# Target rows spread by one-hot products ahead of the edge scores, with the high one-hot rows on ScalarE

## The reference

```python
q = (node_features @ Wq.T + bq).reshape(N, H, D)
k = (node_features @ Wk.T + bk).reshape(N, H, D)
v = (node_features @ Wv.T + bv).reshape(N, H, D)
scores = jnp.sum(q[src] * k[dest], axis=-1) / jnp.sqrt(jnp.float32(D))
scores = scores + attention_mask
seg_max = jax.ops.segment_max(scores, src, num_segments=N)
ex = jnp.exp(scores - seg_max[src])
seg_sum = jax.ops.segment_sum(ex, src, num_segments=N)
weights = ex / seg_sum[src]
weighted = v[src] * weights[:, :, None]
out = jax.ops.segment_sum(weighted, dest, num_segments=N)
```

## Time and profile before

| what | value |
|---|---|
| median of 3 runs | 7013.81 us (7011.34 to 7027.35) |
| the profiled execution, its own time | 7010.85 us |
| its span, first to last instruction | 7009.2 us |
| granted TensorE clock over the span | 0.793 |
| busy: TensorE, VectorE, ScalarE, GpSimd | 4774.6, 4285.0, 2451.2, 4258.3 us |
| first to last instruction of the score stage | 4530.8 to 6053.6 us |

### The profile page before, as it was taken

One profiled execution on the slowest core, in us unless ns is written; L12 is line 12 of the kernel. 1 busy time (PEld: TensorE's weight loads), 2 busy tenths in 40 slices (PEclk: granted clock), 3 DMA queues, 4 the chain that ended last, 5 costly groups with the idle time before them and its releaser, 6 DMA issues. The chain is left out here.

```text
span 7009.2 us, 133354 instructions
## 1 busy us (share of the span) xinstructions
PE 4774.6 (68%) x26165; PEld 3739.8 (53%) x26166; DVE 4285.0 (61%) x13848; ACT 2451.2 (35%) x6084; POOL 4258.3 (61%) x4642
## 2 busy tenths in 40 slices
PE   3666666778868876546887767666666666346557
PEld 2555555557757765435764555444444444235545
DVE  4555556887635543863556757866666666665458
ACT  1555555325652125205313416711111111122149
POOL 3777773003575557667776775477777777347730
PEclk7777777999989988558999967977777777667579
DMA  1222223658969976976875536722222222123358
GB/s 29 72 75 73 74 73 110 196 168 297 342 207 302 314 253 210 343 247 207 268 227 180 179 96 232 248 74 69 70 72 69 69 72 69 49 81 115 85 181 289
DMA packets 616834, 1119.21 MB, mean 160 GB/s; under 512 B 124786, under 2 KB 133392, under 8 KB 616336
## 3 DMA queue, kind: packets, MB, share of 16 engines
q1 hardware_dynamic: 299984, 547.66, 23.3%
q10 hardware_dynamic: 183456, 334.05, 13.8%
q0 software_dynamic: 133280, 236.29, 12.7%
HBM read 675.98 MB, written 441.55 MB: 159 GB/s over the span
## 5 line engine op out<-in xcount | busy, mean ns | idle before, releaser
L520 PE MATMUL agg_bank<-agg_msgs,agg_onehot 128*128 x7840 | 1344.0, 325 | 541.9 <-DVE agg_onehot L450 423.6
L520 PEld LDWEIGHTS agg_bank<-agg_msgs,agg_onehot 128*128 128x128 f32 x7840 | 1161.7, 227 | 777.2 <-issue 773.1
L450 DVE TENSOR_TENSOR agg_onehot<-iota,rel 128x512 f32<-128x512 f32 x1176 | 809.9, 689 | 706.6 <-PE agg_bank L520 271.3
L368 POOL DMA_INDIRECT agg_msgs<-near,agg_rows x784 | 792.7, 1011 | 375.3 <-issue 205.5
L368 POOL DMA_INDIRECT agg_msgs<-y,agg_rows x784 | 784.6, 1001 | 261.6 <-issue 200.4
L564 ACT ACTIVATE agg_kept<-agg_bank 128x512 f32<-128x512 f32 x294 | 175.6, 597 | 1097.9 <-PE agg_bank L520 1084.0
L365 POOL DMA_INDIRECT agg_weight<-weights,agg_rows x392 | 410.7, 1048 | 124.4 <-issue 103.0
L520 PE MATMUL agg_bank<-agg_weighted,agg_onehot 128*128 x1568 | 339.5, 387 | 209.9 <-DVE agg_onehot L450 161.8
L1452 POOL DMA_INDIRECT mlp_xs<-in_x,mlp_rows x392 | 409.2, 1044 | 116.7 <-issue 115.8
L562 ACT ACTIVATE agg_kept<-agg_bank,inv_root 128x128 f32<-128x128 f32 x784 | 224.1, 369 | 721.2 <-PE agg_bank L520 672.1
L1748 POOL DMA_INDIRECT by_source<-score_line,score_places x392 | 389.3, 993 | 125.6 <-issue 117.4
(11 more groups left out here) (344 smaller groups left out, 11942.3 us busy)
## 6 DMA issues: line engine op xcount, KB each, us to landing
sums<-agg_kept ACTq DMA_DIRECT2D x490, 256.0 KB
agg_first<-start ACTq DMA_DIRECT2D x196, 256.0 KB
agg_first<-y ACTq DMA_DIRECT2D x196, 256.0 KB
messages<-mlp_m SPq DMA_DIRECT2D x98, 256.0 KB, 2.1
agg_first<-in_x ACTq DMA_DIRECT2D x98, 256.0 KB
agg_msgs<-messages SPq DMA_DIRECT2D x98, 256.0 KB
l_z<-sums SPq DMA_DIRECT2D x98, 256.0 KB
x<-l_o POOLq DMA_DIRECT2D x98, 256.0 KB
```

Source lines behind the costliest of these rows:

```text
L368: pool.indirect_dma_start(msgs[:, j, :], None, table[:, :], bass.IndirectOffsetOnAxis(ap=rows[:, third, j:j + 1], axis=0)).then_inc(sm[f"g ...
L450: nc.vector.tensor_tensor(onehot[:, j, :, :], k.iota[:, 0:P].unsqueeze(1).to_broadcast([P, Q, P]), k.rel[:, ds(i * (4 * Q) + j * Q, Q)].un ...
L520: t.matmul(bank[:, column[q], :], onehot[:, j, q, :], messages[:, slot[q], :], start=False, stop=True, skip_group_check=True)\
```

## The change

**Setup** also keeps the position of each edge in each step as a row in DRAM (`rel_rows`): TensorE transposes `k.rel` in seven pieces, VectorE copies them as bf16, SyncE stores them. Two more tables tell when an edge group is complete (`edge_done`) and when a node group's buffer is free (`node_left`).

**A new stage** `spread_rows` runs before the scores. It is an aggregation the other way round: it goes through the same 784 steps, with node rows as the loaded ring and edge tiles as the PSUM columns. The positions of a quad's edges are broadcast to all partitions by DMA (bf16, four quads at a time, 512 KB written), VectorE compares them with the partition number, TensorE multiplies the one-hot matrix with the node rows, and ScalarE stores the target row of every edge in a DRAM table. GpSimd, beside this, gathers the source rows of every fourth edge group into another DRAM table.

**The score stage** loads target rows, and the source rows of every fourth group, with plain DMAs on SyncE, ahead of its load of source numbers and of its store. GpSimd gathers sources in three of four groups only. The copy of the turned targets moves from VectorE to ScalarE. The high one-hot rows move from VectorE (one comparison a tile) to ScalarE (two activations a tile: the absolute difference, then Relu of one minus it), as the last step of ScalarE's round.

**Mean products** (`MeanProducts`): VectorE copies the turned rows before it keeps results, where it did so after.

```diff
@@ setup @@
+                sp.wait_ge(sm["rel_rows"], 2)
+                sp.dma_start(rel_rows.rearrange("a (j s e) -> s (a j) e", s=REL_ROWS, e=P), relT[:, :, :]).then_inc(sm["rel_out"], 16)
+                sp.wait_ge(sm["rel_out"], 16)
...
+                v.tensor_copy(relT[:, 0:4, :], pT[0:REL_ROWS, :, :]).then_inc(sm["rel_rows"], 1)
+                v.tensor_copy(relT[:, 4:7, :], pHT[0:REL_ROWS, 0:3, :]).then_inc(sm["rel_rows"], 1)
...
+                for j in range(STEPS // REL_ROWS):
+                    to = pT[0:REL_ROWS, j, :] if j < 4 else pHT[0:REL_ROWS, j - 4, :]
+                    t.transpose(to, k.rel[:, j * REL_ROWS:(j + 1) * REL_ROWS], k.ident[:, :]).then_inc(sm["turned_rel"], 1)
@@ MeanProducts @@
-            for lag, what in ((4, keep), (2, copy)):
+            for lag, what in ((2, copy), (4, keep)):
@@ spread_rows, GpSimd @@
+                    for q in range(Q):
+                        pool.indirect_dma_start(got[:, m, q, :], None, table[:, :], bass.IndirectOffsetOnAxis(
+                            ap=rows[:, m, q:q + 1], axis=0)).then_inc(sm[f"moved{m}"], 16)
+
+                def chunk(i, c):
+                    if not isinstance(i, int) or i * CHUNK + c >= 2:
+                        pool.wait_ge(sm["onehot"], i * (CHUNK * CHUNK) + (c - 1) * CHUNK)
+                    pool.sem_inc(sm["pass_pool"], 1)
+                    pool.dma_start(rel[:, c % 2, :, :], rel_rows[:, ds(i * (CHUNK * CHUNK * Q * P) + c * (CHUNK * Q * P), CHUNK * Q * P)]
+                                   .to_broadcast([P, CHUNK * Q * P])).then_inc(sm[f"rel{c % 2}"], 16)
+
+                def body(i):
+                    for c in range(CHUNK):
+                        chunk(i, c)
+                        if c % 2 == 0:
+                            copy_rows(i, c // 2)
+                        else:
+                            gather(i, c // 2)
...
@@ spread_rows, SyncE @@
+                def load(i, u):
+                    g = i * DEEP + u
+                    sp.wait_ge(sm["summed"], sp.value_load(k.node_left[0:1, ds(g, 1)], min_val=1, max_val=STEPS + SHIFT))
+                    sp.dma_start(nodes[:, u * Q:(u + 1) * Q, :], rows_of(table, g)).then_inc(sm[f"loaded{u}"], 16)
...
+                    for lag, step in ((0, load), (2, arrive)):
@@ spread_rows, VectorE @@
+                        dve.wait_ge(sm["arrived"], arrived)
...
+                        dve.wait_ge(sm["ready"], ready)
...
+                        dve.wait_ge(sm["summed"], i * (2 * CHUNK * Q) + ((c * CHUNK + j) * Q + 1))
+                        nc.vector.tensor_scalar(onehot[:, j, :, :], rel[:, c, j, :].rearrange("p (q e) -> p q e", q=Q), k.pid[:, 0:1], None, ALU.is_equal)\
+                          .then_inc(sm["onehot"], 1)
@@ spread_rows, TensorE @@
+                        pe.wait_ge(sm["onehot"], i * CHUNK + (j + 1))
+                        for q in range(Q):
+                            t.matmul(bank[:, column[q], :], onehot[:, j, q, :], nodes[:, slot[q], :], start=False, stop=True, skip_group_check=True)\
+                             .then_inc(sm["summed"], 1)
@@ spread_rows, ScalarE @@
+                    act.wait_ge(sm["summed"], act.value_load(k.edge_done[0:1, ds(g, 1)], min_val=1, max_val=STEPS + SHIFT))
+                    a.activation(kept[:, u, :, :], bank[:, u * Q:(u + 1) * Q, :], ACT.Copy).then_inc(sm["emptied"], 1)
...
+                        fill(u)
+                    act.dma_start(rows_of(out, g), kept[:, u, :, :]).then_inc(sm[f"written{u}"], 16)
@@ edge_scores, SyncE @@
+                    sp.dma_start(xd[:, u, :, :], rows_of(target_rows, g)).then_inc(sm[f"dst{u}"], 16)
+                    if u == DEEP - 1:
+                        sp.dma_start(xs[:, u, :, :], rows_of(source_rows, g)).then_inc(sm[f"src{u}"], 16)
...
-                    for lag, step in ((0, load_sources), (3, store)):
+                    for lag, step in ((0, load_rows), (0, load_sources), (3, store)):
@@ edge_scores, GpSimd @@
-                    for which, to, sem in ((0, xs, "src"), (1, xd, "dst")):
-                        for q in range(Q):
...
+                    for q in range(Q):
+                        pool.indirect_dma_start(xs[:, b, q, :], None, x3[:, :], bass.IndirectOffsetOnAxis(
+                            ap=rows[:, half, at + q:at + q + 1], axis=0)).then_inc(sm[f"src{b}"], 16)
...
-                        if live(*before_by(i, u, lag, TWICE), TWICE):
+                        if live(*before_by(i, u, lag, TWICE), TWICE) and (lag or u % DEEP < DEEP - 1):
@@ edge_scores, TensorE @@
                 def count(i, u):
+                    pe.wait_ge(sm["hot_hi"], i * DEEP + u + 1)
@@ edge_scores, ScalarE @@
+                    a.activation(xdT[:, u % 2, :, :], pDst[:, :, :], ACT.Copy).then_inc(sm["copied_dst"], 1)
...
+                def make_hot_hi(i, u):
...
+                    for q in range(Q):
+                        last = a.activation(apart[:, q, :], k.iota[:, 0:NT], ACT.Abs, bias=less_hi[:, ds(g * Q + q, 1)])
+                    last.then_inc(sm["apart"], 1)
+                    act.wait_ge(sm["apart"], g + 1)
+                    for q in range(Q):
+                        last = a.activation(hot_hi[:, u % 2, q, :], apart[:, q, :], ACT.Relu, scale=-1.0, bias=k.ones[:, 0:1])
+                    last.then_inc(sm["hot_hi"], 1)
+
                 def body(i, u):
                     for lag, step in ((0, round_off), (0, copy_source), (0, copy_lo), (1, keep)):
...
+                        make_hot_hi(*before_by(i, u, -1))
@@ edge_scores, VectorE @@
-                    v.tensor_copy(xdT[:, u % 2, :, :], pDst[:, :, :]).then_inc(sm["copied_dst"], 1)
...
-                        last = v.tensor_scalar(hot_hi[:, u % 2, q, :], k.iota[:, 0:NT], k.src_hi[:, ds(g * Q + q, 1)], None, ALU.is_equal)
+                        last = v.tensor_scalar(hot_lo[:, u % 2, q, :], k.iota[:, 0:P], k.src_lo[:, ds(g * Q + q, 1)], None, ALU.is_equal)
```

More of the change, by code:

```diff
@@ L1650, in edge_scores @@
+def edge_scores(nc, k, ins, x3, source_rows, target_rows, values, by_source):
+    sm = phase(nc, "score", ["mask", "w", "spread", "rows", "pass_pool", "pass_sp", "turned", "copied_src", "copied_dst", "product", "kept",
                              "multiplied", "reduced", "scored",
-                             "constants", "c", "begun", "hot", "leant", "copied_lo", "rounded", "rest", "looked", "selected", "ranked", "placed", "moved", "counted"] + [f"{s}{u}" for s in ("src", "dst", "stored", "scattered", "line_of") for u in range(DEEP)])
+                             "constants", "c", "begun", "hot", "apart", "hot_hi", "leant", "copied_lo", "rounded", "rest", "looked", "selected", "ranked", "placed", "moved", "counted"] + [f"{s}{u}" for s in ("src", "dst", "stored", "scattered", "line_of") for u in range(DEEP)])
@@ L1964, in body @@
                     if live(*now):
-                        copy_target(*now)
                         take_rest(*now)
```

202 lines of the change are left out of this document (172 added, 30 removed).

## The result

The changed kernel takes 7287.05 us (median of 4 runs, 7281.99 to 7294.84) against 7012.58 for the kernel before: a ratio of 1.0385, 95% interval 1.037 to 1.0401. It is slower, as forecast, but by 274 us and not by 72, and above the range. The profiled execution spans 7293.3 us, 284 more than that of before.

A forecast was written before the change was run, and what follows sets the result against it. GpSimd's descriptor work was taken to bound the score stage, with a 13.8 us loop behind its 15.3. 306 + 9 - 15 - 228 = +72 on 7010.85 gave 7083, stated as 7084 us, range 6945 to 7215.

The forecast's parts named there:

- New stage, 306: Spreading node rows to edges: 196 quads at 1.5 us plus 12 us for barrier, first loads and last stores, costing 306 us.
- Both ends (257 and 404): Limits of the new stage's forecast cost: 1.25 us a quad, and 2.0 for the low clock or a late broadcast.
- The rival of 2.0 us a quad: New stage at the low clock or with late loads: +98 us on the forecast, 7182 us; chance 0.13.
- Score stage, 228: GpSimd stops binding, the loop sets a period of 13.0 us and the stage takes 1305 us, gaining 228 us.
- The chain from keys to look-up: Score stage: ScalarE's row of work from the copy of the keys to the first look-up, 7.2 us (6.5 to 7.8).
- The other half: Score stage loop from first look-up to next keys, four look-ups and four products: 5.8 us (4.7 to 6.5).
- The rival of the high clock: Score stage look-ups and products keep the high clock: 4.7 us, period 11.9, change -35 us, 6978 us; chance 0.33.
- ScalarE's rows at the wrong place: Score stage: high one-hot rows on ScalarE stand between last product and next look-up; 7.5 us becomes 7.2.
- Mean products, -15: Copying turned rows before keeping sums removes TensorE's 53.0 us wait, but DMA caps the gain: -15 us (0 to -40).
- Setup: Serial transposes, copies, small VectorE steps and a DMA with its landing before the stages: 9 us (5 to 15).
- Tables: Rival in the score stage: absolute value and Relu need two table loads a group, over 7250 us; chance 0.02.
- The slower SyncE word: New stage: SyncE announces a node load only after issuing the load two later, so short waits were expected early on.

The follow-up runs named there:

- filled gaps: Changed kernel with unused products in TensorE's two idle gaps of a score-stage period: 7144.67 us, ratio 1.0181, in a set on time.
- late sets: Four of six sets of runs, in which engines waited longer for transfers in most stages; the kernel before itself took 8274 to 8313 us.
- the last fill: Kernel with both one-hot rows beside the look-ups, the rest first and one read a quad, plus 12 unused products before the bias products: 7999.26 us, ratio 0.962.
- the large fills: Changed kernel with 36 unused transposes and 24 unused products in TensorE's two idle gaps, run where transfers were late: 8320.17 and 8229.71 us.

## Why the prediction was wrong

By its own sum, 306 + 9 - 15 - 228 = 72; the profile has 442 + 7 - 5 - 172 and 13 unexplained, 285.

- **New stage, 306 against 442: the step that failed.** The prediction took a quad on TensorE as the weight loads' time plus a gap of 0.21, "1.18 at 2.4 GHz", and let the DMA engines set 1.42. The 0.21 was read from a quad at the low clock, whose 1.78 us of products cover most of what the queue does meanwhile. At the high clock the second of the same rows has 0.66 idle before 0.97. The pace of a quad is the distance of its start from the one before, and with the two quads that stand beside these in the same timeline it was 1.99, 2.19 and 2.44 us:

```profile
6300.40 1.78 PEld L520 LDWEIGHTS agg_bank<-agg_weighted,agg_onehot 128*128 128x128 f32 x8 [1.56 <-issue]
...
6304.58 1.78 PEld L520 LDWEIGHTS agg_bank<-agg_weighted,agg_onehot 128*128 128x128 f32 x8 [0.40 <-issue]
```

The reads themselves had a row in the kernel before, which the prediction doesn't use: the line of the aggregations' reads, whole first aggregation.

```profile
L511 PEldq TENSOR_LOAD <-places x392: 327/333/1143, 1188.0 to 1603.5; - x196
```

The same two reads a quad were there to price, and the row's starts give 2.1 us a quad for 196 of them at a granted clock of 1.00, although VectorE was busy 252 of 300 us there, so that this pace alone wouldn't have named the queue. In the new stage the queue's 0.63 + 0.99 + 0.59 = 2.20 us doesn't come from the clock (quads at the low one are no further apart), from DMA (0.66 busy, and a seventh fewer bytes took off 4.6 us of 442) or from VectorE (its rows are 2.9 us early, and rows 5.6 us early took off 1.9); with fewer or more reads it moved as they did. Both ends (257 and 404) were built from the wrong resources, so the upper one was too low as well. The rival of 2.0 us a quad was nearest in time, for another reason.
- The Trainium skill has a price for it, in "DMA: Bandwidth & Descriptors", section "Latency and other measured facts": a floor of some 600 ns for a tensor_load. By it two reads would be 1.2 us, an estimate. The rows here say 333 ns for four words, 595 for eight and 537 for two, so the page would have overstated this case and still have warned of it.
- **Score stage, 228 against 172: mechanism right, one size off.** The chain from keys to look-up was forecast at 7.2 us by its members and measured 7.27; an activation repeats at 0.51 to 0.54 (2.15 and 2.16 us for four), taken as 0.50. GpSimd stopped binding, as forecast. The other half was mis-sized: 6.38 us against 5.8 (4.7 to 6.5). The prediction saw that the clock falls after two short waits and yet took a value between; in fact 57 of 100 look-up products lasted over 0.45 us, the low clock (0.33 at the high one). 0.58 us on the 96 periods with look-ups is the 56 us that are missing.
- **The rival of the high clock** was priced well, a period of 11.9 (with filled gaps: 12.0), but didn't come by itself. Even with it the change would have lost, 7145 us, because of the new stage.
- **ScalarE's rows at the wrong place**: the prediction said that they stand where the loop passes and that ScalarE's idle time lies beside the look-ups. That is confirmed from both sides: undone, 7.24 instead of 7.27; moved beside the look-ups together with VectorE's, 4.03, and the sign of the whole change turns. What stands next on that way is VectorE's row, with ScalarE's alone moved 5.81 at the median in both late sets.
- **Mean products**, -15 against -5.4. The wait went (TensorE 53.0 us in 94 times, afterwards 3.4 us in 4), but the DMA engines stand at 0.97 of that stage before and after, which was named as the cap. That they are it wasn't tested, and -5.4 itself lies within the scatter of that window.
- **Setup**, 9 against 6.8 (5.1 to 6.8 in the six traces on time). **Tables**: no load in the stage, as expected.
- The slower SyncE word, a late broadcast and the banks' refill, which the prediction had as reasons for 1.5 us and more, were slack: they act through VectorE's rows, and those were early.

Open: what the ScalarE move alone brings on time, what is more than scatter in the 13 us of the untouched stages, what the swap in the mean products is worth, whether the last fill helps, and why some sets are late.

## What to carry to other kernels

When a stage is built from small steps with addresses read from memory, price the instruction queue first: take from the trace the row of the register reads and the interval between first weight loads, not the gap left beside the products. When work is moved to an idle engine, put it where that engine idles; a step in the loop's serial part costs its full length whoever does it, and an order of two steps was worth 358 us here. And ask what a wait's row would say if the named releaser were faster.

## What the hardware showed

- A register read on TensorE's queue took 333 ns for four words, 595 for eight and 537 for two, each at the median, with single ones up to 1.3 to 1.8 us. Two words cost more than four.
- Quads whose addresses are read from memory stood no further apart at the low clock, 2.12 us at 1.2 GHz against 2.24 at 2.4, and where the queue's loop turned it cost 0.65 us more.
- The releaser named in a wait can be one that ended long before: 150 us "for VectorE" with rows 7.6 us early on the mean.
- Products that nobody uses, in the gaps of a latency-bound loop, paid 142 us through the clock (0.75 to 1.00) where transfers were on time.
- In the late sets a faster score stage kept a mean period of 13.9 to 15.2 us whatever the chain's length (16.8 and 17.0 with the large fills), while the new stage, bound by the queue, took 440 to 446 us with its two reads as ever.
